# Pacing the last eight tiles' scatters, and the loads of their rows, by two tiles

## The reference

```python
h  = layernorm(x) * (1 + ca) + sa                  # ca, sa, ga, ... from silu(c) @ wmod, one row per batch
x  = x + ga * attn(h)                              # RWKV-like block: time mix, then channel mix, 7 weights of 512x512
h  = layernorm(x) * (1 + cb) + sb
# ffn(h): one shared expert and 8 routed ones, two per token
shared = (silu(h @ Wsg.T) * (h @ Wsu.T)) @ Wsd.T   # hidden width 704
scores = softmax(h @ Wr.T); w = top2(scores)       # 8 experts
routed = sum over the two best experts e: w_e * (silu(h @ Wg[e].T) * (h @ Wu[e].T)) @ Wd[e].T   # width 352
x  = x + gb * (routed + shared)
```

## Time and profile before

| | |
|---|---|
| median of 3 runs | 1697.74 us (1696.35 to 1703.03) |
| profiled execution, its own time | 1712.11 us |
| span in its trace | 1710.4 us |
| TensorE busy | 1644.5 us, 96% |
| VectorE, ScalarE, GpSimd busy | 1326.6, 769.6, 419.8 us |
| granted TensorE clock, mean | 0.988 |

### The profile page before, as it was taken

One profiled execution on the slowest core, in us unless ns is written; L12 is line 12 of the kernel. 1 busy time (PEld: TensorE's weight loads), 2 busy tenths in 40 slices (PEclk: granted clock), 3 DMA queues, 4 the chain that ended last, 5 costly groups with the idle time before them and its releaser, 6 DMA issues.

```text
span 1710.4 us, 26878 instructions
## 1 busy us (share of the span) xinstructions
PE 1644.5 (96%) x8818; PEld 1427.2 (83%) x8818; DVE 1326.6 (78%) x2553; ACT 769.6 (45%) x1139; POOL 419.8 (25%) x505
## 2 busy tenths in 40 slices
PE   4989999999989999999999979999999999998998
PEld 1667788888778888888888868999999999998987
DVE  5899999998788788787888746677777777776872
ACT  3434433333446464555464413555555555552331
POOL 2344444443322112232323350000000000006740
PEclk8999999999999999999999999999999999999999
DMA  8722222221643534554555687788878888866861
GB/s 296 241 82 91 83 89 90 81 92 62 219 153 131 179 117 149 209 198 178 198 189 182 230 309 250 261 287 300 286 256 284 284 298 273 278 203 221 272 203 38
DMA packets 134300, 335.32 MB, mean 196 GB/s; under 512 B 15852, under 2 KB 15888, under 8 KB 128552
## 3 DMA queue, kind: packets, MB, share of 16 engines
q1 hardware_dynamic: 103904, 248.09, 43.3%
q10 hardware_dynamic: 20040, 52.21, 8.4%
q0 software_dynamic: 10240, 33.56, 5.7%
HBM read 230.21 MB, written 103.60 MB: 195 GB/s over the span
## 4 chain that ended last, share of the span: by engine, by line
PE 74%; DVE 15%; issue 4%; DMA 2%; ACT 2%; POOL 1%; another core or an unknown queue 1%; SPq 0%; DVEq 0%; ACTq 0%; POOLq 0%
PE bank L703 17%; PE bank L705 17%; PE bank L704 17%; PE bank L2435 5%; PE bank L2437 5%; PE bank L2436 5%; PE bank L714 5%; PE bank L2430 2%; DVE stage L1728 2%; DVE mix L1807 1%; DVE xm_lo L1813 1%; PE bank L2419 1%; DVE xm_lo L1734 1%; ACT xm_hi L1407 1%
## 5 line engine op out<-in xcount | busy, mean ns | idle before, releaser
L703 PE MATMUL bank<-gu_hi,ex_x_hl 128*128 128x352 f32 x1080 | 359.8, 333 | 0.1
L705 PE MATMUL bank<-gu_hi,ex_x_hl 128*128 128x352 f32 x1080 | 348.9, 323 | 0.0
L704 PE MATMUL bank<-gu_lo,ex_x_hl 128*128 128x352 f32 x1080 | 348.7, 323 | 0.0
L1294 POOL DMA_INDIRECT raw<-expert_out_rows,out_slots x64 | 76.2, 1190 | 549.2 <-DMA expert_out_rows<-y_rows 523.3
L703 PEld LDWEIGHTS bank<-gu_hi,ex_x_hl 128*128 128x128 f32 x1080 | 203.7, 189 | 0.4 <-issue 0.3
L704 PEld LDWEIGHTS bank<-gu_lo,ex_x_hl 128*128 128x128 f32 x1080 | 204.0, 189 | 0.0
L705 PEld LDWEIGHTS bank<-gu_hi,ex_x_hl 128*128 128x128 f32 x1080 | 203.5, 188 | 0.0
L2435 PE MATMUL bank<-dn_hi,hid_hi 128*128 128x512 f32 x405 | 162.2, 401 | 13.4 <-DVE hid_lo L1906 13.4
L1902 DVE TENSOR_TENSOR hid<-bank,sg_t 128x352 f32<-128x352 f32 x135 | 70.4, 521 | 125.7 <-PE bank L705 104.9
L2437 PE MATMUL bank<-dn_hi,hid_lo 128*128 128x512 f32 x405 | 160.3, 396 | 0.0
L2436 PE MATMUL bank<-dn_lo,hid_hi 128*128 128x512 f32 x405 | 159.3, 393 | 0.0
(11 more groups left out here) (262 smaller groups left out, 3836.5 us busy)
## 6 DMA issues: line engine op xcount, KB each, us to landing
raw<-in_ex_gu SPq DMA_DIRECT2D x40, 1408.0 KB, 6.7
raw<-in_ex_dn SPq DMA_DIRECT2D x40, 512.0 KB, 4.8
ex_x<-expert_in_rows SPq DMA_DIRECT2D x71, 256.0 KB, 6.1
expert_out_rows<-y_rows ACTq DMA_DIRECT2D x71, 256.0 KB, 6.0
h_rows<-h_t SPq DMA_DIRECT2D x64, 256.0 KB, 2.6
h_turned<-h_hl ACTq DMA_DIRECT2D x32, 512.0 KB
ex_x_hl<-h_turned ACTq DMA_DIRECT2D x32, 512.0 KB
x_t<-in_x SPq DMA_DIRECT2D x32, 256.0 KB, 2.7
```

What stands on the lines that cost most here:

```text
L703: pe.matmul(acc, act_hi[i], w_hi[i], start=(i == 0), stop=False)
L704: pe.matmul(acc, act_hi[i], w_lo[i], start=False, stop=False)
L705: last = pe.matmul(acc, act_lo[i], w_hi[i], start=False, stop=(i == chunks - 1))
L1294: pool.indirect_dma_start(rows[:, pair % 2, a, :], None, ys_d, bass.IndirectOffsetOnAxis(ap=out_slots[:, k, n:n + 1], axis=0)).then_inc(ar ...
```

## The change

SyncE loads the eight tiles' rows two at a time: before tiles 26, 28 and 30 it waits until the two before them have landed, and once more behind the last two. GpSimd issues the scatters of two tiles (four scatters) and then waits until all scatters issued so far have landed, before tiles 26, 28 and 30. Nothing else is changed; the same bytes are moved by the same DMAs in the same order on each queue.

```diff
             wait_a2(sp)
             for n in range(24, NT):
+                if n == 28:
+                    sp.wait_ge(sc_last_in[0], 64)
+                elif n % 2 == 0 and n > 24:
+                    sp.wait_ge(sc_last_in[int(n >= 28)], 32)
                 load_last_scattered(n)
+            sp.wait_ge(sc_last_in[1], 64)
             for n in range(FU, FU + 2):
                 load_residual(n)
             sp.wait_ge(*base_vec.done(FU - 1, "base"))
...
             def scatter_last(n):
                 pool.wait_ge(route_vec, (group_of(n) + 1) * ROUTE_OPS)
                 pool.wait_ge(sc_last_in[int(n >= 28)], 64)
+                if n % 2 == 0 and n > 24:
+                    pool.wait_ge(sc_last_out, 32 * (n - 24))
                 for k in range(2):
                     pool.indirect_dma_start(xs_d, bass.IndirectOffsetOnAxis(ap=slots[:, k, n:n + 1], axis=0),
                                             last_rows(n), None).then_inc(sc_last_out, 16)
```

## The result

The changed kernel takes 1708.81 us in the median of 19 runs (1704.32 to 1711.63), the kernel before 1696.61 in the median of 19 (1694.32 to 1703.03). The ratio is 1.0065 with a 95% interval of [1.0058, 1.0072]: about 11 us slower. The forecast was 1698.7.

The account below looks back on a forecast made before the run. TensorE, busy 96% of the span, was taken as the bound, with its 14.0 us hole absent from timed runs. Median 1697.74 plus 1.0 for late residual rows gave 1698.7 us; own range 1694 to 1704, widened to 1688 to 1706.

Parts of the forecast that it names:

- the hole: TensorE idle 12.14 us before unit 32's down products, plus 1.9 at lower clock: 14.0 us, read as absent from timed runs.
- The sign that I called the forecast's clearest: Profile after loses the 14.0 us idle stretch and shows a span near 1698, while timed runs stay where they were.
- Rival A: The 14.0 us idle stretch at unit 32 is in every execution and the change closes it: 1684.7; chance 0.13.
- Step 1, the loads: SyncE's eight loads in four paced rounds: 7.2 + 7.2 + 3.5 + 3.5 = 21.4 us, done at 1012.2.
- Step 2, the residual rows: Tile 15's residual rows issued at 1012.2, landed 1014.9, VectorE needs them at 1013.9: 1.0 us late, all passed to TensorE.
- rival C: Tile 15's residual rows late by the high end, 12.1 us, holding VectorE and TensorE at unit 32: 1710; chance 0.04.
- Step 3, the scatters: GpSimd's four paced rounds from 1005.2, 3.8 issue plus 4.4 landing each: 32.8 us, all landed at 1038.0.
- rival B: Paced scatters landing after 1038.6 delay the first routed rows' loads; at 7.7 us a landing costs 11.6, so 1710; chance 0.08.
- Step 4, SyncE's own path: SyncE's residual issues, store, pads and weight loads before the routed rows: through at 1037.7, or 1040.6 with slow first pads.
- Step 5, the meeting point: Routed rows loaded about 1038.0, landed 1040.5 after 2.5 us, needed by 1041.1 or 1042.1: in time, no cost.

Follow-up runs that it names:

- experiment 1: Kernel before, unedited, profiled again on two chips beside timed runs: profiled 1711.91 us, others 1714.05; profiled 1698.55, others 1696.89.
- residual first: Changed kernel with residual rows of tiles 15 and 16 loaded ahead of the eight tiles' rows; against kernel before 0.999 and 0.9972 with stall, 1.006 without.

## Why the prediction was wrong

**The stall.** "I read the hole as made by the taking of the profile" was wrong as I used it: on one chip the profiled execution and the others have the stall alike, on another neither has it (experiment 1). The difference of 14.4 us that I matched with the hole was, as far as the profiles show, one between two chips, and the missing landing times go with the chip too. Its consequence, that the timed runs of this comparison had nothing to win there, held. The sign that I called the forecast's clearest, a profile after with a span near 1698, did not come: it was 1705.9. Whoever compared only the two profiled executions, 1712.11 and 1707.74, would have read a gain of 4 us in a change that costs 11. By the rule that I set beside it (the Trainium skill, NOTIFIC — the notification-queue block, section 7.1) the profiled execution alone was to stall. The runs do not bear that out: on the chip with the stall the others took 1714.05, and on the other chip a profiled execution with the DMA engines at a share of 0.98 went through without it. They do not refute a part of recording on the chips with the stall either, since the other runs there were recorded in some form too. Rival A holds for one kind of chip: there every run has the level that goes with the stall, and pacing the scatters gives back 9 us. On the kind that was measured here it fails. What holds the engines up is not settled. All that is shown is that in these profiles the stall comes on one kind of chip only, and there only where eight or sixteen scatters go out unpaced.

**Step 1, the loads**, was 21.4 us, and measured 23.1 (991.70 to 1014.80), with the first load 0.9 us later than before. That it came so near is luck: the rounds took 10.4, 4.9, 3.3 and 4.6 us, where I had 7.2, 7.2, 3.5 and 3.5. The first lies above my high end, and the second far below what I took.

**Step 2, the residual rows**, carried these 2.6 us on. They went out at 1014.80 and not 1012.2. The landing of at most 2.7 us and the time of need (1013.84) came as estimated, so the cost was 3.66 us on VectorE, and 3.33 of it reached TensorE, where I had 1.0. This is rival C's place at a third of its price.

**Step 3, the scatters, is the step that failed**, by its size. They were to have landed at 1038.0 and had at 1048.3. Of the 10.3 us, 2.5 are the later start (1007.67 against 1005.2). The issues of the four rounds, first to last start, took 3.85, 4.31, 4.30 and 3.82 us, 16.3 against 15.2. The rest is the landing behind the last start of each round: 4.8, 6.5, 7.3 and 5.8, together 24.4 against four times 4.4. I took 4.4, the median of single scatters of earlier tiles. Issue to landing of the sixteen single scatters, in the changed kernel:

```profile
DMA to landing us min/median/max: 2.9/5.1/7.6
```

So 0.7 us a round is a slower median, 2.8 of the 6.8 us in all. The other 4 come on top because a round waits until all four have landed, and not for a median one. And my argument against rival B, that after 1010 the flood is gone, was wrong. The four rounds as stretches:

```profile
1007.70:1016.30 8.60, 7.78 (x46) 7.05 (x44) 5.17 (x21) 1.13 (x3) 3.88 (x5) 1.00 0.74 251
1016.30:1027.10 10.80, 8.29 (x38) 7.51 (x39) 7.54 (x24) 0.96 (x2) 4.41 (x5) 0.84 0.96 327
1027.10:1038.70 11.60, 11.60 (x69) 10.80 (x68) 5.98 (x12) 1.92 (x4) 4.64 (x5) 1.00 0.87 308
1038.70:1048.30 9.60, 6.98 (x41) 6.24 (x39) 4.49 (x5) 3.29 (x3) 3.86 (x4) 1.00 0.61 220
```

The two longest landings (6.5 and 7.3 us) are those of the second and third round, in which the DMA engines are at 0.96 and 0.87 and SyncE's pads go out; at 0.74 and 0.61 it took 4.8 and 5.8. That the traffic makes the landings long fits these rows, but no run tests it by itself. The estimate by the fit of the Trainium skill, DMA: Bandwidth & Descriptors, was 2.6 us a scatter for the GpSimd path. The least landings on record come near it (2.9 here, 2.7 with one tile at a time); the rounds, at 4.8 to 7.3, do not, and the measurement decides.

**Step 4, SyncE's own path**, was to be through between 1037.7 and 1040.6, and was at 1043.9 (1048.30 less the 4.4 us for the last scatter). The pads took 7.52 and 12.39 us, where I had 8.62 for each. It was not the bound, since the last scatter came 4.4 us later still.

**Step 5, the meeting point**, was right as a mechanism: routed rows are loaded when the last scatter has landed, and turned 2.83 us later (2.5 taken). With the late landing it costs 5.46 and not nothing. That is rival B, with its threshold: it was to decide once scatters land later than 1038.6 (1039.6 by my own 1042.1, which has the lateness of step 2 in it).

**What the sum left out** is the clock behind these two waits. From 1000 to 1065 us TensorE is idle 9.96 us in the changed kernel and 3.81 in the kernel before without the stall, and the granted clock is 0.95 against 1.00:

```profile
1000.00:1065.00 65.00, 55.04 (x304) 50.20 (x303) 35.47 (x84) 16.00 (x22) 16.82 (x16) 0.95 0.79 275
```

```profile
1000.00:1065.00 65.00, 61.19 (x357) 56.01 (x356) 41.22 (x92) 21.11 (x28) 15.96 (x16) 1.00 0.92 325
```

That is 6.2 us of idle time and 0.05 × 65 = 3.2 us of clock (some 0.3 of it in idle time), 9.4 together, where the two spans differ by 1705.9 − 1696.8 = 9.1. The medians differ by 12.2, so one execution of each, on two chips, leaves some of it unexplained. The prediction had such a term for the hole (1.9 us) and none for the waits that its own steps could bring.

**The chances.** B and C had 0.12 together and were priced one at a time. Neither stood alone: both came, each at a part of its high end. "Landing later than 1038.6" had only 0.6 us in hand (1.6 by the 1042.1) over a sum of two landings of loads and four of scatters, the latter at their median; such a margin deserved much more than 0.08.

## What to carry to other kernels

A wait between rounds of DMAs costs one landing a round in which nothing new is issued, and the landing to count is that of the slowest of a round beside whatever else is in flight. Multiply it by the number of rounds before asking whether the last one is in time: one such wait cost nothing here, three cost 6 us (about 12 with the loads paced too), seven cost 16 to 18. And before a stall in a profile is priced, see that the profiled execution and the timed runs come from the same chip; if their times differ by the stall, profile again beside timed runs rather than explain the difference.

## What was not expected of the hardware

The same kernel has a stall of some 14 us on two chips and none on two others. ScalarE and VectorE stand for up to 19.8 us on something that the profile names only `remote`, while TensorE's records show their inputs as done. The DMA engines move 274 GB/s over the 30 us with it, and 366 without. Its cause is open. Pacing the scatters by two removes it on both chips tried, pacing them by four tiles removes a part (one chip), pacing the loads does not remove it. The whole change itself was not run on a chip with the stall. The nearest to it, residual first, was 0.3% faster on one of them, and on the other its interval includes no change.
